# Four score banks beside the scan of a decoder kernel, and four queue orders changed with them

## The reference

```python
def step(params, x):                       # L0_attn: a scan over the 16 batches
    z, y = x @ t_k.T, x @ t_v.T
    grads = jax.grad(loss_fn)(params, z, y)          # loss: mean((z + gelu(z@W1.T+b1)@W2.T + b2 - y)**2)
    new_params = tree_map(lambda p, g: p - LR * g, params, grads)
    return new_params, _recon(new_params, x @ t_q.T)
...
# L0_xattn: 16 heads of width 8 over 77 keys
scores = jnp.einsum('bqhs,bkhs->bhqk', q, k) / np.sqrt(HEAD_DIM)
attn = jax.nn.softmax(jnp.where(context_mask, scores, -inf), axis=-1)
out = einsum('bhqk,bkhs->bqhs', attn, v).reshape(B, Tx, C) @ Wo.T + bo
...
# L0_ffn: top 2 of 8 experts; then L1_attn (self attention with ALiBi), L1_xattn, L1_ffn
```

## Time and profile before

| | us |
|---|---|
| median of 3 runs (lowest, highest) | 710.86 (709.66, 713.04) |
| the profiled execution's own time | 711.03 |
| its span, first to last instruction | 708.9 |
| PE busy | 565.3 (80%) |
| PEld busy | 461.8 (65%) |
| DVE busy | 481.4 (68%) |
| ACT busy | 435.4 (61%) |
| POOL busy | 362.3 (51%) |

### The profile page before, as it was taken

The page is one execution under the profiler, slowest core; times in us unless marked ns, Lnnn a source line. Parts: engine busy times, 40 slices in busy tenths (PEclk is TensorE's granted clock), DMA queues, the critical chain, the costliest instruction groups (busy, mean ns, idle before and its releaser), DMA issues.

```text
span 708.9 us, 18437 instructions
## 1 busy us (share of the span) xinstructions
PE 565.3 (80%) x6129; PEld 461.8 (65%) x6144; DVE 481.4 (68%) x1350; ACT 435.4 (61%) x913; POOL 362.3 (51%) x646
## 2 busy tenths in 40 slices
PE   3796999998997715999849999996987873399990
PEld 1485778776775615999735776764665652299990
DVE  6653468888687452555458999985899986155554
ACT  1453278886684323888526767665786852388872
POOL 5711434665488573566535434321454867355661
PEclk9997569998798756999959999999899997599995
DMA  7749980000000012222190000000000001122216
GB/s 199 223 152 336 337 281 1 2 3 2 9 16 25 24 41 54 77 70 72 38 366 22 2 2 2 2 2 1 2 3 10 25 24 41 51 75 72 72 44 189
DMA packets 42169, 52.66 MB, mean 74 GB/s; under 512 B 11277, under 2 KB 37213, under 8 KB 41789
## 3 DMA queue, kind: packets, MB, share of 16 engines
q1 hardware_dynamic: 33277, 40.04, 18.0%
q0 software_dynamic: 4544, 9.35, 4.0%
q10 hardware_dynamic: 4256, 2.10, 1.0%
HBM read 41.04 MB, written 28.22 MB: 98 GB/s over the span
## 4 chain that ended last, share of the span: by engine, by line
PE 22%; POOL 17%; issue 14%; DVE 13%; DMA 3%; ACT 2%; SPq 0%; POOLq 0%; ACTq 0%; DVEq 0%
POOL yo L1592 10%; PE p_pT L1432 6%; PE p_s L1418 3%; PE p_o L1458 3%; POOL xs L1131 3%; PE p_o L1463 3%; DVE x_prob L1177 3%; DVE x_inv L1184 2%; POOL to_row L1587 2%; DVE x_top L1167 2%; PE p_s L1409 2%; DMA back<-yo 1%; PE p_s L1700 1%; ACT x_pT L1325 1%; DMA xs<-send,x_index 1%
## 5 line engine op out<-in xcount | busy, mean ns | idle before, releaser
L1592 POOL DMA_INDIRECT yo<-context,to_row x78 | 76.0, 975 | 65.6 <-POOL to_row L1587 51.4
L1654 ACT ACTIVATE context<-pack 128x1156 f32 x78 | 90.6, 1166 | 26.5 <-DVE context L1626 17.6
L1700 PE MATMUL p_s<-xT_f,context 128*128 128x128 f32 x624 | 85.8, 282 | 0.0
L1700 PEld LDWEIGHTS p_s<-xT_f,context 128*128 128x128 f32 x624 | 79.3, 199 | 0.0
L1131 POOL DMA_INDIRECT xs<-send,x_index x64 | 64.1, 1001 | 22.1 <-issue 15.9
L1619 DVE TENSOR_SCALAR context<-p_s,context 128x128 f32<-128x128 f32 x156 | 47.5, 346 | 34.1 <-PE p_s L1700 34.1
L1325 ACT ACTIVATE x_pT<-p_pT 128x512 f32<-128x512 f32 (+1 forms) x96 | 48.8, 524 | 28.4 <-PE p_pT L1432 26.1
L1661 ACT ACTIVATE context<-p_s,context 128x128 f32<-128x128 f32 x156 | 47.6, 355 | 21.6 <-PE p_s L1700 12.0
L1432 PE MATMUL p_pT<-sq,x_prob 128*128 128x128 f32 x320 | 54.4, 297 | 6.3 <-ACT x_pT L1325 5.5
L1167 DVE TENSOR_REDUCE x_top<-p_s 128x12 f32<-128x924 f32 (+2 forms) x48 | 46.9, 1006 | 15.9 <-PE p_s L1418 15.8
L1177 DVE TENSOR_TENSOR x_prob<-p_s,x_top 128x768 f32<-128x768 f32 (+2 forms) x96 | 50.0, 576 | 0.1
(11 more groups left out here) (257 smaller groups left out, 1498.6 us busy)
## 6 DMA issues: line engine op xcount, KB each, us to landing
xs<-in_blank SPq DMA_DIRECT2D x2, 8707.5 KB, 42.8
pack<-in_pack SPq DMA_DIRECT2D x16, 578.0 KB, 9.2
context<-xs SPq DMA_DIRECT2D x78, 64.5 KB, 1.8
back<-yo SPq DMA_DIRECT2D x6, 256.0 KB, 4.7
back<-yo ACTq DMA_DIRECT2D x6, 256.0 KB, 5.6
yo<-context,to_row POOLq DMA_INDIRECT x78, 2.3
x<-in_x SPq DMA_DIRECT2D x4, 256.0 KB, 4.4
xs<-send,x_index POOLq DMA_INDIRECT x64, 2.4
```

The lines of the kernel that those rows point to most:

```text
L1592: nc.gpsimd.indirect_dma_start(yo[:, :], bass.IndirectOffsetOnAxis(to_row[:, n % NY, :], 0), y[:, n % NY, :], None).then_inc(y_stored[n % ...
L1654: nc.scalar.activation(ws[:, n % NW, :], pack[:, bass.ds(e, 1), :].rearrange("p a w -> p (a w)"), ACT.Copy).then_inc(ws_ready, 1)
L1700: ins = mm(p_h[n % 2][k // 2][:, P * (k % 2):P * (k % 2 + 1)], ws[:, n % NW, P * k:P * (k + 1)], xT[:, n % 2, :], start=True, stop=True)
```

## The change

- Scores beside the scan go into four banks of four heads: three of `p_s`, and the first of `p_pT`, where P is also turned. The semaphore between strips goes.
- `score` waits for ScalarE's copies of the turned P of the batch before the last; `tp0` of a batch waits for VectorE's shift of the next batch's last four heads.
- VectorE's `max` and `shift` are each cut in two steps: B (heads 12 to 15, the shared bank) and A (the other twelve). B's two come first in the round, then `scale`, then A's two, then `choose` and the scan's `eTa`. Before, `shift` stood behind `da` and `address`.
- ScalarE's `exp` moves ahead of the routing's copy `c_rturn`; TensorE's `eT` moves ahead of `po`.

```diff
-FIRST_PE = ((3, "score"), (0, "aT"), (1, "aq"), (0, "a"), (4, "tp0"), (5, "po"), (0, "eT"), (2, "turn_in"), (1, "gw2"), (4, "tp1"), (1,
+FIRST_PE = ((3, "score"), (0, "aT"), (1, "aq"), (0, "a"), (4, "tp0"), (0, "eT"), (5, "po"), (2, "turn_in"), (1, "gw2"), (4, "tp1"), (1,
     "out"), (0, "e_"), (0, "dh"), (4, "tp2"), (8, "rank"), (2, "project"), (0, "g2"), (0, "g1"), (7, "rturn"), (4, "mix"), (0, "g1b"), (7,
     "rlogit"))
-FIRST_DVE = ((5, "scale"), (8, "choose"), (3, "max"), (0, "eTa"), (5, "res"), (1, "w2n"), (0, "slope2"), (0, "slope3"), (1, "comb"), (0,
-    "da"), (8, "address"), (3, "shift"), (1, "count"), (0, "w1n"), (5, "rcount"), (0, "b1n"), (0, "w2Tn"))
-FIRST_ACT = ((0, "hT"), (1, "hq"), (0, "acopy"), (4, "pT0"), (2, "c_turn"), (0, "h"), (4, "pT1"), (0, "e"), (4, "pT2"), (2, "c_q"), (7,
-    "c_rturn"), (3, "exp"), (7, "c_rlg"))
+FIRST_DVE = ((3, "maxB"), (3, "shiftB"), (5, "scale"), (3, "max"), (3, "shift"), (8, "choose"), (0, "eTa"), (5, "res"), (1, "w2n"), (0, "slope2"), (0, "slope3"), (1, "comb"), (0,
+    "da"), (8, "address"), (1, "count"), (0, "w1n"), (5, "rcount"), (0, "b1n"), (0, "w2Tn"))
+FIRST_ACT = ((0, "hT"), (1, "hq"), (0, "acopy"), (4, "pT0"), (2, "c_turn"), (0, "h"), (4, "pT1"), (0, "e"), (4, "pT2"), (2, "c_q"), (3, "exp"), (7, "c_rturn"), (7, "c_rlg"))
...
-        banks = ((range(0, 6), 0), (range(6, 12), 2), (range(12, 16), 3))
-        strips = [[(0, 4, 0, 0)], [(0, 2, 0, 4), (2, 4, 1, 0)], [(0, 4, 1, 2)], [(0, 4, 2, 0)]]
+        banks = [p_s[:, 0, :], p_s[:, 1, :], p_s[:, 2, :], p_pT[:, 0, :]]
+        lone = p_pT[:, 0:1, 0:GW].rearrange("p g (h k) -> p g h k", k=T)
+        pieces = {"A": (0, HG * (NG - 1), p_s[:, 0:NG - 1, 0:GW].rearrange("p g (h k) -> p g h k", k=T)), "B": (HG * (NG - 1), NH, lone)}
...
+        def find_top(piece):
+            h0, h1, scores = pieces[piece]
+
+            def run(b, p):
+                dve.wait_ge(scored, FIRST + b + 1)
+                nc.vector.tensor_reduce(top[:, h0:h1].rearrange("p (g h) -> p g h", h=HG), scores, AX.X, ALU.max).then_inc(top_done, 1)
+            return run
+
+        def shift(piece):
+            h0, h1, scores = pieces[piece]
+
+            def run(b, p):
+                dve.wait_ge(top_done, TOP_0 + PIECES * b + (1 if piece == "B" else PIECES))
...
-                act.wait_ge(shifted, SHIFTED_0 + SHIFTS * b + PIECES * (part_no + 1))
+                act.wait_ge(shifted, SHIFTED_0 + SHIFTS * b + SHIFTS - NPARTS + part_no + 1)
...
+            if beside:
+                wait(pe, pT_sb, NS * (b - 1))
...
+            for g in range(NG):
                 r = slice(STRIP * g, STRIP * (g + 1))
-                if beside and g == 1:
-
-                    pe.wait_ge(strips_scored, 2 * (b + 1))
...
+                last = mm(banks[g][:, 0:GW], qT[r, p, :], kT[r, p, :, :].rearrange("p h k -> p (h k)"), start=False, stop=True)
             last.then_inc(scored, 1)
...
+                    if beside and g == 0 and b + 1 < NB:
+                        pe.wait_ge(shifted, SHIFTS * (b + 1) + NPARTS)
```

More of the change, by code:

```diff
@@ L710 @@
 SCAN_SEMS = ("set_up", "acts", "a", "a_sb", "sq", "th", "hT", "h", "slope", "num", "eT", "eT_sb", "e", "e_sb", "dh", "da", "g1", "g2", "g1b", "g2b",
-             "b1_new", "w2T_new", "w1_new", "w2_new", "aq", "hqT", "out", "added", "zero", "safe", "den", "strips_scored")
+             "b1_new", "w2T_new", "w1_new", "w2_new", "aq", "hqT", "out", "added", "zero", "safe", "den")
 def scan_work(own):
@@ L1162, in count_x @@
             s.end()
[L1164 to L1178, removed]
+        def find_top(piece):
[8 more added lines that the diff above has]
+                dve.wait_ge(top_done, TOP_0 + PIECES * b + (1 if piece == "B" else PIECES))
+                wait(dve, p_turned, NS * (FIRST + b - 1))
+                if not own and FIRST + b == 0:
+                    dve.wait_ge(set_up, 1)
+                for part in parts:
+                    k0, k1 = part[2:]
+                    nc.vector.tensor_tensor(prob_of(p, part)[:, h0:h1, :].rearrange("p (g h) k -> p g h k", h=HG), scores[:, :, :, k0:k1],
+                                            top[:, h0:h1].rearrange("p (g h) -> p g h", h=HG).unsqueeze(3).to_broadcast([P, (h1 - h0) // HG, HG, k1 - k0]),
                                             ALU.subtract).then_inc(shifted, 1)
+            return run
         def scale_out(b, p):
@@ L1392, in alibis @@
         def alibis(b, p):
-            for bank, (hs, strip) in enumerate(banks):
-                mm(p_s[:, bank, 0:len(hs) * T], m["ident_bf"][:, :], m["alibi"][:, hs[0]:hs[-1] + 1, :].rearrange("p h k -> p (h k)"), start=True, stop=False)
+            for g in range(NG):
+                mm(banks[g][:, 0:GW], m["ident_bf"][:, :], m["alibi"][:, HG * g:HG * (g + 1), :].rearrange("p h k -> p (h k)"), start=True, stop=False)
         def score(b, p):
@@ L1401, in score @@
                 pe.wait_ge(m["masks_placed"], 64 * NG)
-            for bank, (hs, strip) in enumerate(banks):
-                to = p_s[:, bank, 0:len(hs) * T]
+            if beside:
+                wait(pe, pT_sb, NS * (b - 1))
+            for g in range(NG):
+                to, r = banks[g][:, 0:GW], slice(STRIP * g, STRIP * g + mask_rows)
                 if mask:
-                    r = slice(STRIP * strip, STRIP * strip + mask_rows)
                     mm(to.rearrange("p (h k) -> p h k", k=T), ones_bf[r, :],
-                       m[mask][r, b, :].unsqueeze(1).to_broadcast([mask_rows, len(hs), T]), start=True, stop=False)
+                       m[mask][r, b, :].unsqueeze(1).to_broadcast([mask_rows, HG, T]), start=True, stop=False)
                 elif b:
-                    mm(to, m["ident_bf"][:, :], m["alibi"][:, hs[0]:hs[-1] + 1, :].rearrange("p h k -> p (h k)"), start=True, stop=False)
+                    mm(to, m["ident_bf"][:, :], m["alibi"][:, HG * g:HG * (g + 1), :].rearrange("p h k -> p (h k)"), start=True, stop=False)
             pe.wait_ge(q_sb, FIRST + b + 1)
             pe.wait_ge(k_sb, FIRST + b + 1)
-            for g in (0, 2, 3, 1) if beside else range(NG):
+            for g in range(NG):
                 r = slice(STRIP * g, STRIP * (g + 1))
-                if beside and g == 1:
-                    pe.wait_ge(strips_scored, 2 * (b + 1))
[L1417 to L1421, removed]
+                last = mm(banks[g][:, 0:GW], qT[r, p, :], kT[r, p, :, :].rearrange("p h k -> p (h k)"), start=False, stop=True)
             last.then_inc(scored, 1)
```

19 lines of the change are left out of this document (8 added, 11 removed).

## The result

The changed kernel takes 734.51 us (median of four runs, 732.58 to 735.85) against 710.26 us for the kernel before on the same chip: ratio 1.035, 95% interval 1.031 to 1.039. Forecast was 722.4, with a range up to 734.0. The side was right, the size was not: +24.3 us where +11.4 was worked out, and the time lies just outside the range.

What follows compares the result with a forecast made beforehand. The prediction took PE's product queue to bound the scan and cross attention stage. Round terms of -2.4, +1.0, +7.0, +1.7, -0.8, +2.4, +0.9, +2.1 and -0.5 gave +11.4 on 711.03: 722.4 us, range 714.5 to 734.

Steps and rivals of the forecast that it cites:

- PE's score block: Scores beside the scan: four strips in four banks take 0.80 us instead of 1.71, saving PE 0.91 a round.
- VectorE's block: Maxima, shifts and scale between score and eT addition: 4.37 us, so the eT addition starts at S + 5.27.
- the two waits: PE idles before the turn of e, for the eT addition, and before rlogit, for c_rturn; plain round 10.22 us against 8.84.
- the turn of e (which needs the eT addition, 0.34 behind its start): In PE's queue beside the scan: the turn of e starts 0.34 us behind the eT addition, at S + 5.61.
- rival C: PE, idle 2.3 of 10.2 us, loses its clock in full-clock rounds; two more low stretches give 733 us; chance 0.09.
- cost nothing: Outside the scan and cross attention stage, order, buffers and wait values stay as they are, so no time is added.
- The product queue itself is the bound: In rounds 8 to 11 before the change, PE is busy 8.56 of 8.84 us and its queue sets the round.
- Rival D: PE stays the bound, round 7.93, about 697 us, if the eT addition can start by S + 3.8; chance 0.08.
- 0.83 the routing copy: With the exponential ahead of c_rturn, rlogit starts at 9.90 instead of 9.07: 0.83 us of a plain round's +1.38.
- B: c_rturn is in time, so rlogit does not wait: eight rounds at 0.83 us less, 715.7 us; chance 0.13.
- E: Nothing measurable: no rlogit wait, full -4.2 us in the low-clock rounds, round 17 unharmed; 712 us; chance 0.10.
- F: Strips in four banks still go one by one: 15 rounds at 0.91 us on top, 736 us; chance 0.02.

Runs made afterwards that it cites:

- res_early: The changed kernel with the residual moved ahead of VectorE's shift of the twelve heads: 724.88 us, ratio 1.020.
- out_late: The changed kernel with the scan's out product moved behind the turn of e and dh in PE's queue: 736.4 us, ratio 1.041.
- filled: The changed kernel with four extra products a round, results unused, in PE's idle stretch ahead of out: 731.43 us, ratio 1.030.
- filled_again: The changed kernel with four unused products ahead of out, run a second time beside the unaltered changed kernel: 728.77 us, ratio 1.029.
- exp_alone: The kernel before, three banks, with only the exponential moved ahead of c_rturn: 727.09 us, ratio 1.020.
- neither: The changed kernel with the exponential back behind c_rturn and the twelve heads' shift back behind da: 707.85 us, ratio 0.999.
- late_logits: The changed kernel with the twelve heads' shift back behind da and the routing's logits and their copy one round later: 703.00 us, ratio 0.990.
- no_exp: The changed kernel with only ScalarE's exponential back behind c_rturn: 723.09 us, ratio 1.018.

## Why the forecast was right in side and wrong in size

- **PE's score block, VectorE's block, the two waits**: right, each within 0.05 us (0.77 for 0.80, eT addition at 5.32 for 5.27). From the last turns to the next mask product the changed kernel needs 152.97 - 148.79 = 4.18 us; the forecast's own terms give 10.22 - 6.02 = 4.20.
- **"the turn of e (which needs the eT addition, 0.34 behind its start)": the first step that failed.** It starts 148.53 - 147.61 = 0.92 behind. It waits for `w2n`, and the `out` ahead of it for the residual; both stand behind the eT addition on VectorE. I listed the first wait of the turn of e and not its third, and I put `out` at about 4.5 as if its residual were done, though the change had just moved that residual behind the whole block. The row of round 12 before showed `out` released by the residual, 171.03 - 170.41 = 0.62 behind the eT addition; the turn of e followed at 171.33, the same 0.92 behind. Price: 0.48 us at the last turns (6.50 for 6.02; the `dh` between them was 0.15 quicker than the earlier trace rows had it), 10.68 for 10.22. Over rounds 5 to 11, 14 and 15 that is about 4.2 us. `res_early` and `out_late` show the parts.
- **The clock: the second step that failed**, rival C, which had a chance of 0.09. It was to need gaps like the 2.02 us of round 12; "my gaps are of 0.7 at most" was wrong by the term above, by counting each gap alone, and by the forecast's own wait ahead of `rlogit` (9.90 - 9.07 = 0.83). The rows have 0.17, 0.24, 1.30 and 0.86 us in one round. Three rounds fell to low clock, 2 us each: 12.71 - 10.75, 12.69 - 10.68, 12.76 - 10.67, together 6 us. `filled` and `filled_again` show that PE's idle time is the cause in this kernel. The table above goes with the longest gap, but so few profiles are no rule, and `exp_alone`, whose only gap in a plain round is one of 0.86 us, had low clock all the same in its one profile. Which length or sum of gaps is safe, and why one round falls and not its neighbour, stays open. The Trainium skill, TensorE: Matmul & The Clock Gate, Part 1, says that the gate follows how busy the engine has recently been; `filled` agrees, and I gave the rule too little weight.
- **The rest of the miss**: round 12 took 16.67 for 15.4, with PE idle 4.80 us where 3.9 was forecast (the eT addition at S + 8.82 for 8.51, the turn of e at 10.01 for 8.85, which is the first step's miss at low clock), +1.3; round 16 took 10.73 for 9.3, at a clock of 0.84, +1.4; the time behind round 17 was 1.3 longer and not 0.5 shorter, +1.8. From there to the rank of the last group (251.82 before, 274.02 after) it is in fact 0.9 shorter. But a stretch of self attention that the change does not touch (371.97 to 384.06 us before, 394.85 to 408.65 after) takes 13.80 us and not 12.09, at a mean clock of 0.76 and not 0.93, and the first experts (274.58 to 350.32 before, 296.87 to 373.60 after) take 76.73 and not 75.74, at 0.96 and not 0.98. So "cost nothing" outside the stage held for the work and not for the clock; one profile of each kernel does not show whether that comes of the change or of chance. Rounds 3 and 4 gave 3.35 back (2.4 forecast, and 0.25 later at the start of round 3), round 13 1.74 (0.8 forecast). Sum: 4.2 + 6.0 + 1.3 + 1.4 + 1.8 - 0.7 - 0.9 = 13.1, against 24.4 - 11.4 = 13.0.
- **"The product queue itself is the bound": the third step that failed**, without a price in this forecast. By the forecast's own terms `neither`, whose eT addition starts at S + 4.10 (149.02 - 144.92), should have had 4.10 + 1.78 + 2.34 = 8.22 (an estimate: 1.78 from the eT addition to grad_w1, 2.34 from there to the next S), and it has 8.84. `late_logits`, with the same order on VectorE, has 8.52. PE at 8.56 busy of 8.84 was at most one of two limits of nearly equal length; the other is ScalarE's loop, in which no engine is busy throughout. Rival D's round of 7.93 rested on PE alone. Its condition, the eT addition by S + 3.8, is met in no run, so it was not tested.
- **The swap of `eT` and `po` is worth nothing**: right in a round (10.68 with and without).
- **No drain behind a table load**: right. The exponential starts 151.10 - (149.81 + 1.28) = 0.01 us behind its load, and the load 0.02 behind the copy ahead of it. By the Trainium skill, ScalarE: Activation LUTs, What ACT_TABLE_LOAD costs, 1.38 us more per switch would have been due; no run here shows it.
- **"0.83 the routing copy"**: right in kind, 0.14 too much: `no_exp` gives 10.68 - 9.99 = 0.69.
- **Rivals B, E, F**: B needed `rlogit` without a wait and has 0.86. E falls with it. F falls with the score block of 0.77.

## What to carry to other kernels

When a block is moved ahead on one engine, list every semaphore that each later instruction of the other queues waits for, not only its data, and ask of each whether its signal stands behind the moved block. A round length that nearly equals one engine's busy time is no proof that this engine alone sets it: look for a loop of hand-overs of the same length, and shorten both at once, as `late_logits` does. And price idle time of TensorE twice: as time, and as the clock that it can take from the products behind it.

## What the runs showed of the hardware that was not expected

- The granted clock fell in rounds whose longest idle stretch of PE is 1.30 us, and in `exp_alone` in rounds with one of 0.86. In round 7 of the changed kernel PE had stood still for 0.16 and 1.30 us ahead of the fall; the part at low clock has it busy throughout. The two parts of that round:

```profile
118.83:125.00 6.17, 4.57 (x41) 3.39 (x40) 5.60 (x16) 4.80 (x12) 3.00 (x7) 0.99 0.01 3
125.00:131.54 6.54, 6.54 (x69) 5.37 (x69) 2.42 (x14) 3.71 (x7) 2.51 (x6) 0.50 0.01 3
```

- Work whose result nobody reads made the kernel faster: four products, 9.26 - 8.12 = 1.14 us of PE in each round, took 6.9 us off the median side by side (735.69 and 728.77).
